# A second accumulating transfer per tile and three passes for every group of layer 1, in a two-layer interaction network

## The reference, cut to what matters

```python
z = einsum('bhd,bmd->bhmd', x0, prev).reshape(b, h*m, d)   # products of two fields
cur = relu(einsum('bpd,pn->bnd', z, W))                    # 128 maps
prev = cur                                                 # layer 1: h*m = 32*32, layer 2: 32*128
...
result = sum(concatenate([cur_1, cur_2], axis=1), axis=-1) # then 3 dense layers
```

## Time and profile before

| what | value |
|---|---|
| time, median of 2 runs | 859.55 us (858.24 to 860.85) |
| the profiled execution's own time | 856.8 us |
| its span, first to last instruction | 855.0 us |
| PE busy / DVE / ACT / POOL | 847.2 / 787.5 / 679.0 / 661.5 us |
| granted TensorE clock, mean | 0.996 of full speed |

### The profile page before, as it was taken

One profiled execution on the slowest core, in us unless ns is written; L12 is line 12 of the kernel. 1 busy time (PEld: TensorE's weight loads), 2 busy tenths in 40 slices (PEclk: granted clock), 3 DMA queues, 4 the chain that ended last, 5 costly groups with the idle time before them and its releaser, 6 DMA issues.

```text
span 855.0 us, 13830 instructions
## 1 busy us (share of the span) xinstructions
PE 847.2 (99%) x3527; PEld 663.0 (78%) x3527; DVE 787.5 (92%) x2394; ACT 679.0 (79%) x2231; POOL 661.5 (77%) x677
## 2 busy tenths in 40 slices
PE   8999999999999999999999999999999999999998
PEld 3777887777787777778777778877777877777874
DVE  4889999999999999999999999999999999999992
ACT  3778888788888888888888888887888888888862
POOL 5567888888788887777887878888878898867680
PEclk9999999999999999999999999999999999999998
DMA  5888666687766668776667775666877676784430
GB/s 169 194 201 208 159 135 139 163 184 170 178 138 140 155 162 187 164 163 157 132 162 164 181 167 128 146 160 163 183 170 154 131 164 164 161 186 84 91 74 1
DMA packets 55093, 131.05 MB, mean 153 GB/s; under 512 B 8036, under 2 KB 19140, under 8 KB 55013
## 3 DMA queue, kind: packets, MB, share of 16 engines
q0 software_dynamic: 22384, 68.70, 43.5%
q1 hardware_dynamic: 31090, 58.79, 22.7%
q10 hardware_dynamic: 1539, 2.67, 1.0%
HBM read 59.35 MB, written 4.20 MB: 74 GB/s over the span
## 4 chain that ended last, share of the span: by engine, by line
PE 92%; DMA 4%; DVE 2%; POOL 1%; ACT 1%; issue 0%; SPq 0%; DVEq 0%; ACTq 0%; POOLq 0%
PE t_act L797 13%; PE t_act L799 13%; PE t_act L798 13%; PE t_dve L797 13%; PE t_dve L799 13%; PE t_dve L798 13%; PE acc L764 6%; PE acc L769 5%; DMA prod<-prod 2%; PE acc L773 1%; DMA x_rows<-emb 1%; DVE prod L575 1%; POOL prod L303 1%; DVE prod L586 0%; PE t_act L875 0%
## 5 line engine op out<-in xcount | busy, mean ns | idle before, releaser
L418 ACT ACTIVATE prod<-t_act,weigh 128x128 f32<-128x128 f32 x2048 | 575.5, 371 | 102.7 <-PE t_act L799 96.9
L575 DVE SCALAR_TENSOR_TENSOR prod<-t_dve,weigh,prod 128x128 f32<-128x128 f32 x1792 | 481.0, 342 | 8.5 <-PE t_dve L799 6.4
L303 POOL TENSOR_TENSOR prod<-prod 128x512 f32<-128x512 f32 x254 | 298.8, 1176 | 29.6 <-DMA prod<-prod 19.0
L797 PE MATMUL t_act<-w_hi,cur_hi 128*128 128x512 f32 x512 | 212.4, 415 | 0.0
L799 PE MATMUL t_act<-w_hi,cur_lo 128*128 128x512 f32 x512 | 199.8, 390 | 0.0
L798 PE MATMUL t_act<-w_lo,cur_hi 128*128 128x512 f32 x512 | 199.6, 390 | 0.0
L797 PE MATMUL t_dve<-w_hi,cur_hi 128*128 128x512 f32 x512 | 199.6, 390 | 0.0
L799 PE MATMUL t_dve<-w_hi,cur_lo 128*128 128x512 f32 x512 | 199.3, 389 | 0.0
L798 PE MATMUL t_dve<-w_lo,cur_hi 128*128 128x512 f32 x512 | 199.1, 389 | 0.0
L287 POOL DMA_DIRECT2D prod<-prod x127 | 119.8, 943 | 90.2 <-ACT prod L418 46.0
L268 POOL DMA_INDIRECT emb<-table_dram,all_ids x128 | 156.7, 1224 | 39.9 <-issue 31.7
(11 more groups left out here) (92 smaller groups left out, 566.5 us busy)
## 6 DMA issues: line engine op xcount, KB each, us to landing
prod<-prod POOLq DMA_DIRECT2D x127, 512.0 KB, 5.1
x_shift<-x_rows SPq DMA_DIRECT2D x62, 512.0 KB, 6.6
x_pair<-x_rows SPq DMA_DIRECT2D x94, 128.0 KB, 4.5
x_same<-x_rows SPq DMA_DIRECT2D x31, 256.0 KB, 3.3
x_rows<-emb SPq DMA_DIRECT2D x64, 64.0 KB
w_raw<-w_dram ACTq DMA_DIRECT2D x8, 256.0 KB, 4.2
emb<-table_dram,all_ids POOLq DMA_INDIRECT x128, 3.0
w_raw<-wt_dram SPq DMA_DIRECT2D x2, 512.0 KB, 7.5
```

Of the source, the lines that this page charges most:

```text
L303: nc.gpsimd.tensor_tensor(src[:, dst, :], src[:, dst, :], src[:, other, :], ALU.add).then_inc(folded, 1)
L418: last = nc.scalar.activation(prod[i][:, HEADS * a + j, :], t_act[n % ARING][:, j * MAPS:(j + 1) * MAPS], ACT.Copy, scale=weigh[p][:, i, h ...
L575: nc.vector.scalar_tensor_tensor(dst, src, w, dst, ALU.mult, ALU.add).then_inc(added, 1)
L797: nc.tensor.matmul(bank[:, :], cur_hi[p][:, cols], w_hi[:, w], start=True, stop=False)
```

## The change

Two things at once.

1. After `halve(c, i)` and `fold(c, i-1)` POOL runs the new `halve_again(c, i)`: it waits for the transfer that `halve(c, i)` issued, and issues a second accumulating transfer, places 4 to 7 onto 0 to 3. `fold` waits for that one, and has one step less: the 128x512 addition of L303 is gone, the 128x256 one and L309 stay. (The last tile's `last_fold` on DVE is as before.)
2. All four groups of layer 1 go in three `fp32r` passes from chunk 3 on. ACT rounds z of groups 0 and 1 too (`round_first`, 128x1024, after tile 2 of chunk c for chunk c+2; `round_last` moves from after tile 2 to after tile 3). DVE makes two more low parts (`lower_first`, 128x512 each, at the end of a chunk). PE gives `layer1_half` when groups 0 and 1 are read. Some small buffers are laid over others to make room.

```diff
-FOLDS = {8: [(slice(0, 4), slice(4, 8)), (slice(0, 2), slice(2, 4))],
+FOLDS = {8: [(slice(0, 2), slice(2, 4))],
...
+            def halve_again(c, i):
+                pool.wait_ge(halved[i % 2], (c * (TILES // 2) + i // 2 + 1) * 16)
+                nc.gpsimd.dma_start(prod[i][:, 0:4, :].rearrange("x h n -> x (h n)"),
+                                    prod[i][:, 4:8, :].rearrange("x h n -> x (h n)"),
+                                    accum_op=ALU.add).then_inc(halved_again[i % 2], 16)
+
             def fold(c, i, p):
...
-                pool.wait_ge(halved[i % 2], (c * (TILES // 2) + i // 2 + 1) * 16)
+                pool.wait_ge(halved_again[i % 2], (c * (TILES // 2) + i // 2 + 1) * 16)
...
                         fold(c, i - 1, p)
                     elif c > 0:
                         fold(c - 1, TILES - 1, 1 - p)
+                    halve_again(c, i)
...
+            def round_first(c, p):
+
+                act.wait_ge(z_ready, c * 3 + 1)
+                act.wait_ge(layer1_half, c - 1)
+                nc.scalar.activation(z_hi[:, 0:WHOLE, :], z[p][:, 0:WHOLE, :], ACT.Copy).then_inc(first_rounded, 1)
...
-                    if i == 2 and not ((c == 0 or c + 2 >= CHUNKS)):
+                    if i == 2 and 0 < c < CHUNKS - 2:
+                        round_first(c + 2, p)
+                    if i == 3 and 0 < c < CHUNKS - 2:
                         round_last(c + 2, p)
...
+            def lower_first(c, p):
+                dve.wait_ge(first_rounded, c - LEAD + 1)
+                for g in range(WHOLE):
+                    nc.vector.tensor_tensor(z_lo[:, g, :], z[p][:, g, :], z_hi[:, g, :].bitcast(fp32),
+                                            ALU.subtract).then_inc(first_lo_ready, 1)
...
                 if more2:
                     products(c + 2, p, 1)
+                    if c > 0:
+                        lower_first(c + 2, p)
...
-                    if g < WHOLE or g < GROUPS and c <= 2:
+                    if g < GROUPS and c < LEAD:
...
+                        nc.tensor.matmul(acc1[:, :], v_hi[:, g, :], z_hi[:, g, :], start=g == 0, stop=False)
+                        nc.tensor.matmul(acc1[:, :], v_lo[:, g, :], z_hi[:, g, :], start=False, stop=False)
+                        last = nc.tensor.matmul(acc1[:, :], v_hi[:, g, :], z_lo[:, g, :], start=False, stop=False)
+                        if g == WHOLE - 1:
+                            last.then_inc(layer1_half, 1)
```

More of the change, by code:

```diff
@@ L15 @@
 GROUPS = 4
-SPLIT = 2
-WHOLE = GROUPS - SPLIT
+WHOLE = GROUPS // 2
 BANK = 512
@@ L69, in dlrm_tower @@
         z = [sb(f"z{p}", [128, GROUPS, COLS]) for p in range(2)]
-        z_hi = sb("z_hi", [128, SPLIT, COLS], f32r)
-        z_lo = sb("z_lo", [128, SPLIT, COLS], f32r)
+        z_hi = sb("z_hi", [128, GROUPS, COLS], f32r)
+        z_lo = sb("z_lo", [128, GROUPS, COLS], f32r)
         z_last = [sb(f"z_last{p}", [3 * FIELDS, COLS]) for p in range(2)]
@@ L74, in dlrm_tower @@
         v = sb("v", [128, GROUPS, MAPS])
-        v_hi = sb("v_hi", [128, SPLIT, MAPS], f32r)
-        v_lo = sb("v_lo", [128, SPLIT, MAPS], f32r)
+        v_hi = sb("v_hi", [128, GROUPS, MAPS], f32r)
+        v_lo = sb("v_lo", [128, GROUPS, MAPS], f32r)
         v_last = sb("v_last", [3 * FIELDS, MAPS])
@@ L94, in dlrm_tower @@
         pool1 = sb("pool1", [128, TILES, CHUNKS * QUARTERS])
-        ctx_sb = sb("ctx_sb", [CTX, BATCH])
-        wt1_ctx = sb("wt1_ctx", [CTX, TOP1])
         bt1_sb = sb("bt1_sb", [128, T1])
@@ L109, in dlrm_tower @@
         apart2 = x_shift[0].rearrange("x h (i c q) -> x h i c q", i=TILES, q=QUARTERS)
+        room = 2 * TOP1 + T1 * TOP2
+        ctx_sb = w_raw[0:CTX, room:room + BATCH]
+        wt1_ctx = w_raw[0:CTX, room + BATCH:room + BATCH + TOP1]
         h2 = w_raw[:, 2 * TOP1 + T1 * TOP2:2 * TOP1 + T1 * TOP2 + T2 * BATCH].rearrange("n (f b) -> n f b", f=T2)
-        pool1_hi, pool1_lo = (sb(f"pool1_{half}", [128, BATCH], f32r)[:, :] for half in ("hi", "lo"))
+        pool1_hi, pool1_lo = z_hi[:, 0, :], z_lo[:, 0, :]
         h1 = z[0]
@@ L150, in dlrm_tower @@
         z_rounded = sem("z_rounded")
+        layer1_half, first_rounded, first_lo_ready = sem("layer1_half"), sem("first_rounded"), sem("first_lo_ready")
         pair_rounded, z_lo_ready = sem("pair_rounded"), sem("z_lo_ready")
@@ L161, in dlrm_tower @@
         halved = [sem(f"halved{p}") for p in range(2)]
+        halved_again = [sem(f"halved_again{p}") for p in range(2)]
         folded = sem("folded")
@@ L239, in chunk @@
                 sp.dma_start(x_shift[p][:, WHOLE:GROUPS, :].rearrange("p g c -> p (g c)"),
-                             shifted(WHOLE, SPLIT)).then_inc(x_rest[p], 16)
+                             shifted(WHOLE, GROUPS - WHOLE)).then_inc(x_rest[p], 16)
             def top_loads():
@@ L394, in round_pair @@
                 act.wait_ge(layer1_done, c)
-                nc.scalar.activation(z_hi[:, :, :], z[p][:, WHOLE:GROUPS, :], ACT.Copy).then_inc(pair_rounded, 1)
+                nc.scalar.activation(z_hi[:, WHOLE:GROUPS, :], z[p][:, WHOLE:GROUPS, :], ACT.Copy).then_inc(pair_rounded, 1)
             def relu2(c, p):
@@ L523, in products @@
                                             ALU.mult).then_inc(z_ready, 1)
+            def lower_first(c, p):
[3 more added lines that the diff above has]
+                                            ALU.subtract).then_inc(first_lo_ready, 1)
             def lower_pair(c, p):
                 dve.wait_ge(pair_rounded, c - 2)
-                for k in range(SPLIT):
-                    nc.vector.tensor_tensor(z_lo[:, k, :], z[p][:, WHOLE + k, :], z_hi[:, k, :].bitcast(fp32),
+                for g in range(WHOLE, GROUPS):
+                    nc.vector.tensor_tensor(z_lo[:, g, :], z[p][:, g, :], z_hi[:, g, :].bitcast(fp32),
                                             ALU.subtract).then_inc(z_lo_ready, 1)
@@ L618, in _ @@
             dve.wait_ge(v_ready, 1)
-            nc.vector.tensor_copy(v_hi[:, :, :], v[:, WHOLE:GROUPS, :]).then_inc(v_ready, 1)
+            nc.vector.tensor_copy(v_hi[:, :, :], v[:, :, :]).then_inc(v_ready, 1)
             dve.wait_ge(v_ready, 2)
-            nc.vector.tensor_tensor(v_lo[:, :, :], v[:, WHOLE:GROUPS, :], v_hi[:, :, :].bitcast(fp32),
+            nc.vector.tensor_tensor(v_lo[:, :, :], v[:, :, :], v_hi[:, :, :].bitcast(fp32),
                                     ALU.subtract).then_inc(v_ready, 1)
@@ L763, in layer1 @@
                             pe.wait_ge(z_ready, c * 3 + 3)
-                        nc.tensor.matmul(acc1[:, :], v[:, g, :], z[p][:, g, :], start=g == 0, stop=False)
+                        last = nc.tensor.matmul(acc1[:, :], v[:, g, :], z[p][:, g, :], start=g == 0, stop=False)
+                        if g == WHOLE - 1:
+                            last.then_inc(layer1_half, 1)
                     elif g < GROUPS:
[L766 to L769, removed]
+                        if g < WHOLE:
+                            pe.wait_ge(first_lo_ready, (c - LEAD) * WHOLE + g + 1)
+                        else:
+                            pe.wait_ge(z_lo_ready, (c - LEAD) * WHOLE + g - WHOLE + 1)
+                        nc.tensor.matmul(acc1[:, :], v_hi[:, g, :], z_hi[:, g, :], start=g == 0, stop=False)
+                        nc.tensor.matmul(acc1[:, :], v_lo[:, g, :], z_hi[:, g, :], start=False, stop=False)
+                        last = nc.tensor.matmul(acc1[:, :], v_hi[:, g, :], z_lo[:, g, :], start=False, stop=False)
+                        if g == WHOLE - 1:
+                            last.then_inc(layer1_half, 1)
                     else:
```

## The result

The changed kernel takes 1190.03 us (median of 2 runs, 1186.34 to 1193.73) against 859.55 us: 1.385 times the time, 95% interval 1.377 to 1.393. The forecast was 1125 us, range 1010 to 1200.

The account below looks back on a forecast made before the run. PE bounds the kernel before (25.14 us a chunk); after the change POOL would, its waits, issues, gathers and last step summing to 34.0 us a chunk. With start, last chunks and tail: 1125 us, range 1010 to 1200.

Parts of the forecast that it names:

- four landings: On POOL, four times a chunk from the first transfer's start to its landing: 22.8 us.
- waking up: On POOL, waking up four times a chunk after the waits: 0.3 us.
- four second issues: On POOL, issuing the second transfer four times a chunk at 0.9 us each: 3.6 us.
- four gathers: On POOL, gathers for chunk c+3, 1.224 us and 0.25 idle each, now on the path: 5.9 us a chunk.
- L280: POOL's step at the chunk's end (L278 before the change), 1.28 us and 0.1 behind it: 1.4 us a chunk.
- one landing of four collides with SP's reads: One of four transfers stays long beside SP's reads; 22.8 us taken, near the lower window of 22.3 to 24.8.
- The tail: From the last first transfer's start on POOL to the kernel's end: 33.3 us, in place of 31.5 after L309.
- Where PE stands still: PE, with 24.8 us of work, stands still 9 us of each chunk, waiting for ACT's banks; ACT for L309.
- The clock rival: PE's waits halve its clock; decides only if over 37% of its work runs lower; mostly 1150 to 1300 us; chance 0.05.
- The first rival: Not slower: the new wait fits POOL's idle time, landings 3.4 us each; 849 to 860 us; chance 0.04.
- DVE's chunk: Two more subtractions, some 1.2 us, take DVE's chunk to 24.9, or 25.6 where it is busiest; within 2%.
- PE's side: Layer 1's groups 0 and 1 go from 1.72 to 1.36 us a chunk: 10.4 us less over 29 chunks.

Follow-up runs that it names:

- e4: Changed kernel without the second transfer, POOL's 128x512 addition put back, still waiting for each tile's transfer at the change's early point: 1020.33 us (one run).
- e3: Changed kernel with the second transfer issued a tile later, behind the next tile's first transfer, and the fold another tile later: 909.09 us, 1.061.
- e2: Kernel before plus only the second accumulating transfer with its wait, layer 1 as before: 1188.63 us, 1.384.
- e1: Kernel before with only layer 1 changed to three passes for all groups; one transfer per tile and POOL's addition kept: 867.87 us, 1.011.
- e7: Changed kernel, but from chunk 3 on SP's reads of the shifted layouts fetch 16 columns in place of 512 (or 1024): 1076.42 us, 1.254.
- e6: Changed kernel with the middle pass of layer 2 (high part by the weights' low part) left out: 1178.86 us, 1.373.
- e9: Kernel before with three of layer 1's four groups in three passes from chunk 3 on, group 0 in plain float32: 856.61 us, 1.000.
- e12: As e10, but layer 1 as in the kernel before: 878.56 us, 1.024.
- e10: As e3, with the relu of layer 2 and the sums behind it also one tile later: 883.96 us, 1.030.
- e11: As e10, with group 0 of layer 1 in plain float32: 876.24 us, 1.025.

## Why the prediction was right

**The mechanism** was the one forecast: the wait for a transfer just issued makes POOL's chunk longer than PE's. e4 shows it by adding only the wait (152 us), e3 by issuing the same transfers without the early wait (281 us less), e2 that layer 1 has no part in it. The wait and the second transfer are not separate costs: the 170 us from e4 to the change count only because the early wait puts them on POOL's path; without it the second transfer and the later fold together cost 41 us (e3 against e1).

**The size** is in the range, 65 us over the forecast, and the term that was mis-sized is the four landings, 22.8 us forecast and 25.4 measured. By the rows of the chunk at 505 us:

| term | forecast, us a chunk | measured |
|---|---|---|
| four landings of L289 | 22.8 | 4.7 + 2 x 6.2 + 8.3 = 25.4 |
| waking up | 0.3 | 26.5 - 25.4 = 1.1 |
| four second issues | 3.6 | 3.0 |
| four gathers | 5.9 | 4.7 |
| L280 | 1.4 | 1.7 |
| sum | 34.0 | 35.9 |

I argued that one landing of four collides with SP's reads and that a longer chunk would ease it. Two of four collide, because the reads (524.4 to 529.4 us) start just after the third L289 and reach into the fourth, and the tiles that POOL handles in that stretch are the ones with nothing else between their transfers. e7 priced it: 114 us, more than the whole miss. I had the larger value at hand and took the one near the smaller. The window of the earlier trace rows was a mild one: over chunks 3 to 28 of the kernel before, the four landings sum to 23.6 us in the mean. The forecast would have fitted e4, whose medians sum to 22.5: what it missed is that the second transfer and its place change which landings collide. The first chunks are longer too (41 and 39 us), which the sum left out. Two other terms were too high, the second issues and the gathers, and hid 1.8 us a chunk of the error. The tail was right: 1191.9 - 1158.6 = 33.3 us from the last L289 to the end, as forecast.

**Where PE stands still** was wrong in detail. I had it wait for ACT's banks and so for `side`. ACT waited for `side` before `prod` only 36.4 us; PE waited 257.7 us at layer 1's last matmul for `lower_last`, the step at the end of POOL's chunk that I had costed as 1.4 us on POOL and not followed to its reader. With POOL two tiles behind, it is the first result of POOL that PE misses. It did not change the time, since POOL's chain does not run through PE: `halve` waits for DVE or ACT for 5.7 us in the whole run. The profile's own chain that ended last does pass through PE, ACT and DVE in each chunk, but by the row of 531.17 us that names DVE; with that row read as the transfer it stays on POOL, and e6, which takes 156 us of PE's busy time away and gains 11, agrees.

**The clock rival** happened and did not decide, as its condition said. The clock falls once in a chunk, but PE is busy for 911.1 us in place of 847.2 - 10.4 = 836.8; by my estimate the 74 us more mean that some 9% of its work ran at the lower level, far under 37%. And e6, with a third less of layer 2's matmuls and a still lower clock, changed the time by under 1%. The row that the rival rested on was read too freely: from 835 to 840 us PE was busy for 4.74 of 5 us, so it shows the lower clock, but no matmuls that stand apart. The rows after the change show it: a wait of 8.65 us, and then matmuls at 0.50. The gaps the Trainium skill (TensorE: Matmul & The Clock Gate, "HAM oscillation — how this bites in real kernels") tells of are here, in every chunk. The trace agrees with it on the fall (0.50 behind each wait); what differs is the price, since here the lost time lies inside POOL's longer chunk.

**The first rival** is refuted: the shortest L289 still took 4.6 us. The estimate of 3.2 us by the Trainium skill's fit (DMA: Bandwidth & Descriptors, "Anatomy of one DMA — SWDGE (gpsimd) path") is met by no accumulating transfer of this size; the 256 KB ones took 3.2 us at best and 3.3 in the median. The advice of the same page (section "Rules for kernel authors") to issue early and wait late is what e3 bears out, 909 us against 1190.

**Layer 1.** The forecast let DVE's chunk end between 24.9 and 25.6 us and called the sum "within 2%"; e1 has 1.1% more, the upper end: DVE's slack did not carry two subtractions. PE's side was near: the six passes of groups 0 and 1 take 1.46 us in e1 (from 515.40 us) where 1.36 were forecast. e9 shows the trade as even: one group moved, no gain, no loss.

## What to carry to other kernels

An engine that issues a transfer and has in-order work to do should not wait for it before that work. Its chunk then becomes the landings plus all that does not lie beside them (35.9 us here), and the price is what this exceeds the chunk of the old bound by (25.1). It appears on an engine that the profile shows less busy than before (here 48%, down from 77%). Price such a wait by the landings in the stretch where it will stand, those that collide with other traffic included, and add what stands behind it in the program. Moving an addition to a transfer saved nothing here, where POOL had idle time; and even with the wait well placed, 2.4% stayed lost (e12), with ACT waiting for the buffer and slower landings.

## What the runs showed of the hardware

- Between the landing of a transfer and the start of the POOL instruction that waits for it lie 0.3 us (1.1 us for the four of the chunk at 505 us).
- An issue lasts 0.85 to 1.2 us in the rows, but POOL's next instruction, another issue included, begins 0.6 us after its start (522.97 to 523.57); a gather begins 1.2 us after (514.09 to 515.29).
- An accumulating transfer of 512 KB from SBUF to SBUF lands after 4.5 us at best (the kernel before), one of 256 KB after 3.2 (the change); with DMA busy for 0.9 (e10, e11, e12) they take 6.4 to 7.2 us in the median.
- The granted clock went to 0.51 of full in a stretch in which PE was busy for 3.33 of 10 us, after a wait of 8.65 us, and was back at 0.98 in the next, in which PE was busy throughout.
